# Moving one head's position matmuls from the 2nd to the 9th chunk of each attention step, and splitting a transpose from its reciprocal

## The reference

```
att     = softmax(einsum('nqd,nkd->nqk', qm, km))        # 32 (batch, head) blocks, each 2048 x 2048, d = 16
pos     = rel_bias[buckets]                               # 2048 x 2048 per head, the same for both batches
att_out = einsum('nqk,nkd->nqd', att + pos, vm)
```

## Time and profile before

| what | value |
|---|---|
| time of the profiled execution | 3223.95 us |
| its span | 3222.2 us |
| PE busy, whole span | 2937.4 us (91%) |
| DVE busy, whole span | 2141.4 us (66%) |
| ACT busy, whole span | 1781.4 us (55%) |
| stretch of the 32 steps | about 988 to 2329 us |
| PE, DVE, ACT busy from 1200 to 2200 us | 999.55, 952.91, 836.58 us of 1000 |

### The profile page before, as it was taken

One profiled execution on the slowest core, in us unless ns is written; L12 is line 12 of the kernel. 1 busy time (PEld: TensorE's weight loads), 2 busy tenths in 40 slices (PEclk: granted clock), 3 DMA queues, 4 the chain that ended last, 5 costly groups with the idle time before them and its releaser, 6 DMA issues. The chain is left out here.

```text
span 3222.2 us, 55594 instructions
## 1 busy us (share of the span) xinstructions
PE 2937.4 (91%) x20650; PEld 1758.2 (55%) x20650; DVE 2141.4 (66%) x3379; ACT 1781.4 (55%) x3477; POOL 770.3 (24%) x1336
## 2 busy tenths in 40 slices
PE   5788999996979999999999999999876588899999
PEld 2566888883434333333333333333343267688888
DVE  4445555443459999999999999999234444555554
ACT  3345333331215888888888888888724244433333
POOL 2642310000132222222222222211102354230000
PEclk7899999997878999999999999999988699999999
DMA  7795211104575444445555555442043489421110
GB/s 218 232 274 177 65 40 31 33 24 165 195 140 58 56 56 57 56 57 61 61 61 61 61 61 61 54 48 34 9 150 109 121 267 284 124 69 34 30 30 20
DMA packets 446796, 301.75 MB, mean 94 GB/s; under 512 B 170291, under 2 KB 421272, under 8 KB 446536
## 3 DMA queue, kind: packets, MB, share of 16 engines
q1 hardware_dynamic: 412616, 214.33, 34.0%
q0 software_dynamic: 33920, 83.93, 8.2%
HBM read 183.01 MB, written 118.78 MB: 94 GB/s over the span
## 5 line engine op out<-in xcount | busy, mean ns | idle before, releaser
L1460 DVE TENSOR_REDUCE mx_ha<-s_ps_ha 128x2 f32<-128x1024 f32 x1024 | 1243.4, 1222 | 73.2 <-PE s_ps_ha L1367 66.4
L1526 ACT ACTIVATE probs_ha<-s_ps_ha 128x512 f32<-128x512 f32 x2048 | 1108.3, 595 | 192.6 <-PE s_ps_ha L1378 58.0
L1367 PE MATMUL s_ps_ha<-ks_ha,qs_ha 48*128 48x512 f32 x2048 | 759.5, 455 | 18.6 <-DMA ks_ha<-parts_d 13.3
L1378 PE MATMUL s_ps_ha<-qs_ha,ks_ha 50*128 50x512 f32 x2048 | 749.8, 446 | 0.8 <-ACT probs_ha L1526 0.2
L1389 PE MATMUL o_ps_ha<-probs_ha,vs_ha 128*32 128x256 f32 (+1 forms) x7936 | 646.8, 398 | 0.9 <-DVE oT_ha L1487 0.9
L1367 PEld LDWEIGHTS s_ps_ha<-ks_ha,qs_ha 48*128 48x128 f32 x2048 | 313.2, 190 | 449.6 <-DVE mx_ha L1460 372.2
L882 ACT ACTIVATE probsT_a<-pT_ps_a 128x512 fp32r<-128x512 f32 x256 | 146.4, 597 | 424.2 <-PE pT_ps_a L756 424.2
L1389 PEld LDWEIGHTS o_ps_ha<-probs_ha,vs_ha 128*32 128x32 f32 x7936 | 157.0, 108 | 359.0 <-issue 185.5
L1378 PEld LDWEIGHTS s_ps_ha<-qs_ha,ks_ha 50*128 50x128 f32 x2048 | 305.3, 185 | 33.0 <-ACT probs_ha L1526 32.5
L1318 POOL TENSOR_TENSOR onorm_ha<-oT_ha,rinv_ha 128x256 f32<-128x256 f32 x32 | 19.8, 619 | 982.5 <-DVE rinv_ha L1490 982.5
L799 DVE TENSOR_REDUCE nmax_a<-s_ps_a 128x1 f32<-128x2048 f32 x64 | 146.7, 2292 | 162.3 <-PE s_ps_a L745 162.3
(11 more groups left out here) (201 smaller groups left out, 3927.5 us busy)
## 6 DMA issues: line engine op xcount, KB each, us to landing
xs_p<-xs_d SPq DMA_DIRECT2D x282, 128.0 KB
ys_d<-y_p SPq DMA_DIRECT2D x66, 512.0 KB, 3.6
qs_ha<-parts_d SPq DMA_DIRECT2D x192, 128.0 KB, 6.3
ks_ha<-parts_d SPq DMA_DIRECT2D x192, 128.0 KB, 7.2
parts_d<-parts_hp POOLq DMA_DIRECT2D x32, 512.0 KB, 3.1
leaf_w_p<-in_wa SPq DMA_DIRECT2D x6, 1048.0 KB
leaf_w_p<-in_wb SPq DMA_DIRECT2D x6, 1040.0 KB
xs_d<-y_p SPq DMA_DIRECT2D x6, 1024.0 KB, 12.1
```

Source lines behind the costliest of these rows:

```text
L1367: nc.tensor.matmul(s1_ps[:, e % BANKS, :], qs[0:QKROWS, n % SLOTS, c, :], ks[0:QKROWS, n % SLOTS, g * 4:(g + 1) * 4, :].rearrange("p c t - ...
L1378: nc.tensor.matmul(out, ks[LOW:LOW + KR, n % SLOTS, c, :], qs[LOW:LOW + KR, n % SLOTS, g * 4:(g + 1) * 4, :].rearrange("p c t -> p (c t)") ...
L1460: nc.vector.reduce_max(mx[:, at:at + 2], s1_ps[:, e % BANKS:e % BANKS + 2, :], AX_X).then_inc(s1_free, 1)
L1526: nc.scalar.activation(probs[:, (n + c) % (LATE + 1), g * 512:(g + 1) * 512], s2_ps[:, turn % TURNS, :], ACT.Exp).then_inc(s2_free, 1)
```

## The change

`POS_AT` goes from 1 to 8, so that positions come behind chunk 8 of each step instead of behind chunk 1. This one number sets PE's order, ACT's (the copy comes behind the activations of chunk 8) and the turns of `s2_ps`. SP's order stays as it is written, but the store's wait is met later. And `turn_out` is made in two pieces on DVE: the transpose stays behind the maxima of pair 30, and the reciprocal now comes behind the maxima of the following pair.

```diff
-        POS_AT = LATE - 1
+        POS_AT = RC // 2
...
                     scan_max(n, e)
                     if n > 0 and e // 2 <= MSTEPS:
                         max_parts(n - 1, e // 2)
-                    if n >= 2 and e == TURN_AT:
-                        for i in range(2):
-                            turn_out(n - 2, i)
+                    if n >= 2 and 0 <= e - TURN_AT < 4:
+                        turn_out(n - 2, (e - TURN_AT) // 2)
```

## The result

The kernel with the change takes 3250.73 us (median of six runs, 3246.49 to 3254.17), against 3223.59 us for the kernel before in the runs beside them (3219.32 to 3226.6). The ratio is 1.0084, with a 95% interval of 1.0072 to 1.0097: +27.1 us. The forecast was 3246.3 us, +22.3 us over the profiled execution of before, in a range of 3238 to 3255.

The account below looks back on a forecast made before the run. The prediction took PE as the bound, with no slack in a step to hide a wait. 29 steps x 0.77 us = +22.3 us, other terms zero, on 3223.95 us gave 3246.3 us, range 3238 to 3255.

Parts of the forecast that it names:

- PE is the bound: Middle stage: PE's work fills each 41.83 us step; it takes 1.23 us a unit, DVE could go at 1.13.
- The rival by which DVE sets the pace: Middle stage: DVE is the bound, PE's wait is eaten by time lost anyway; no change, 3224 us; chance 0.05.
- The price of the wait: Chunk 2, steps 1 to 29: PE waits for the uncovered transpose, +0.77 us a step, +22.3 us in all.
- Positions behind chunk 8: PE, each step: positions take the same 2.20 us there, difference zero, bounds -5 and +6 us; DVE starved about 1.3 us.
- The reciprocal: DVE, one reduction later: POOL gets it about 1.2 us later, zero cost; at most 1.2 us once.
- SP's queue: SP: the later store stands ahead of `load_m`, still clears by 4 us, and costs nothing.
- the prediction's rival: SP: maxima's DMAs wait until position stores land, nearly 5 us late; 73 us on top, 3319 us; chance 0.04.
- Step 0: First step, at the lower clock: positions gain 1.6 us, work moved forward loses as much; zero, ends -1.6 and +1.6.
- The clock as a rival: PE, chunk 2: the repeated 0.70 us idle lowers the clock, 80 us more, 3326 us; chance 0.02.

Follow-up runs that it names:

- Experiment 6: The changed kernel with DVE's transpose one pair of reductions later (TURN_AT 32); 3376.19 us, ratio 1.0491 to the kernel before.
- experiment 8: The changed kernel with the 512-column products of a block's first chunk behind all four scans of chunk 2; 3222.89 us, ratio 1.0 to the kernel before.
- Experiment 5: The changed kernel with DVE's transpose one pair of reductions sooner (TURN_AT 28); 3253.22 us, ratio 1.0097 to the kernel before.
- Experiment 1: The kernel before with only the positions moved behind chunk 8, transpose and reciprocal together as before; 3275.81 us, ratio 1.0072.
- 9: The changed kernel run once more, unaltered, beside the last group of runs; 3287.35 us, ratio 1.0094 to the kernel before.
- Experiment 2: The changed kernel with positions back behind chunk 1, so only the split of transpose and reciprocal remains; 3249.93 us, ratio 0.9998 to the kernel before.
- Experiment 7: The changed kernel with positions behind chunk 12 instead of 8; 3293.78 us, ratio 1.0205 to the kernel before.
- Experiments 3: The changed kernel with positions behind chunk 1 in step 0 alone, behind chunk 8 in the others; 3270.46 us, ratio 1.0057 to the kernel before.
- experiment 4: The kernel before with positions behind chunk 8 in step 0 alone; 3256.61 us, ratio 1.0012.
- 10: The changed kernel with 512-column products behind all four scans of chunk 2 and step 0's positions behind chunk 1; 3255.94 us, ratio 0.9998 to the kernel before.

## Why the prediction was right, and where a size was off

**PE is the bound: right.** The wait of 0.71 us lengthened every step. Experiment 6 lengthens the wait by 1.23 us and the undisturbed step by 1.26; experiment 8 removes the wait and the step is back. The rival by which DVE sets the pace is out, and with it the order of engines by the Trainium skill's rule in "Perfetto Trace Analysis", section Identifying the Most-Contended Engine: weight loads are busy 387 of 1000 us and DVE 933, and still it was PE's waits that were paid. The section names MFU, the share of the peak arithmetic rate, beside the weight loads; it is not worked out for any run here. Experiment 5 shows where DVE's margin ends: 0.61 us of waiting at that place is more than it can make up ahead of PE's next scans.

**The price of the wait: right at its place, a little large for the step.** The stretch grew by 4.65 - 3.87 = 0.78 us, as read from step 30. The step grew by 0.69 only. The other 28 units of a step take (42.52 - 5.88 - 2.20)/28 = 1.230 us, with 5.88 us from the first scan of chunk 2 to that of chunk 4, where they took (41.83 - 5.10 - 2.20)/28 = 1.233. So the term is 19.9 us instead of 22.3. Why a unit is 3 ns shorter stays open. Experiment 1 has it without the split, and experiments 1, 8 and 9 show where: there a unit takes 1.230 us from the positions to the next chunk 2 and 1.233 from chunk 2 to the positions.

**Positions behind chunk 8: right.** 2.20 us for 2.20. DVE's starving there was mis-sized, 2.20 us for 1.3, and cost nothing.

**The reciprocal, SP's queue: right.** Experiment 2 shows the split at nothing. The store is out of the way by almost 7 us, not the 4 that I had reckoned. Experiment 7 shows that SP's order costs something with the positions behind chunk 12, mostly 0.45 us a step; the landing of the stores, on which the prediction's rival hung, holds nothing back.

**Step 0: the term that was mis-sized.** I had taken zero, "ends -1.6 and +1.6", on the ground that positions moved out of the slow stretch gain what the work moved into it loses. The unspoken assumption was that the clock would rise at the same moment. It doesn't have to. In the profile it rose 21 us later and cost 8.3 us; over the timed runs the term is 27.1 - 19.9 = about 7 us. Experiments 3 and 1, which differ in step 0 and in the split (nothing, by experiment 2), are 5.3 us apart; experiment 4 alone costs 4.5 us (interval from 0.3 to 7.8, by 0.0001 and 0.0024 of 3252). That late positions cause a cost is borne out by the two tables above together: 7.0 us is left over on the mean with them late and 0.2 with them early. Its size is not the same in each kernel: experiment 8, with them late too, has 3.2 us, which cannot be told from nothing. It is not settled what in PE's work lifts the clock: units with scans, scores and products keep PE busy all the time and didn't lift it for 20 us and more, and in three profiles it rose 8.1 to 11.3 us into the step, long before the late positions.

The sum came out near in part by luck: the two errors have opposite signs, 2.4 us too much for the waits and 7 too little for step 0. Without the late clock the time would have been 2.4 us below the forecast, in its range too.

**The clock as a rival: not here.** At 0.71 us of idle PE in each step the granted clock stayed at 1.00 for the whole window. The Trainium skill, "TensorE: Matmul & The Clock Gate", section A second HAM failure mode: psum-queue depth-cycling, warns of brief idle times between groups of matmuls. The changed kernel shows no such thing, but experiment 6, with 1.94 us in the same place, does, and so does experiment 7, with 1.16 to 1.32 us at the start of a step.

**A faster version.** None was found. Experiments 8 and 10 bring the changed kernel back to the kernel before and not below it, as PE's own work fills the step either way.

## What to carry to other kernels

Work that sits between the last use of a buffer and its reuse may be cover for another engine's step; before moving it, count from the release to the next use without it. Where a loop has a few iterations that lack the covering work (the last heads here), their rows give the price beforehand, to a tenth of a microsecond. A move within a loop also moves work in its first iteration, and if that one runs before the clock has risen, its cost must be worked out by itself, with a wide range.

## What the runs showed of the hardware that I had not expected

- A PE without a gap can stay at the lower clock for long: in the changed kernel from 1000 to 1017.8 us, with 10.00 us of 10 busy in each window and a granted clock of 0.50 up to the rise.
- A longer wait costs out of proportion, by the clock. With 0.71 us of idle PE in each step the granted clock was 1.00 throughout. With 1.94 us it fell in 15 of the steps 1 to 29, to 0.96 on the mean of 1200 to 2200 us, single steps took 52 to 55 us instead of 43.78, and the timed runs lost 126 us over the changed kernel where the wait alone explains 37. In experiment 7 it fell after idle starts of 1.16 to 1.32 us, and not after one of 2.06: the length of one wait does not decide it alone.
- The two stores of positions took 0.99 us to issue into a queue with nothing ahead of them, and 3.33 us behind twelve loads. The eight DMAs of the maxima took 5.0 us to issue in most steps of experiment 7 and up to 6.0 in others.
